# Two more weight blocks in flight at the first hand-over of a weight stream, and an output bias added on TensorE

## What is computed

```
x = x + gat2(elu(gat1(layernorm(x))))          # gat1: 8 heads of 768, W1 (768, 6144); gat2: W2 (6144, 768)
t = layernorm(x)
probs = softmax(t @ Wg + bg)                   # 8 experts, the best one is used
comb = one_hot(argmax(probs)) * max(probs)
h = gelu(t @ W1[e] + b1[e])                    # W1 (8, 768, 3072)
y = h @ W2[e] + b2[e]                          # W2 (8, 3072, 768)
ffn = sum over e of y * comb[e]
v = clip(ffn @ Wv + bv, -3, 3)                 # one number for each node
scores = sigmoid(t @ Wm + bm); mask = scores >= k-th largest
gr, gi = diagonal of (T(v) - i I)^-1           # tridiagonal, by continued fractions
feats = clip(stack(gr, gi) * mask, -10, 10)
out = x + ffn + bk_scale * (feats @ Wo + bo)
```

## Time and profile before

| | |
|---|---|
| median of 3 runs | 510.85 us (510.09 to 513.81) |
| the profiled execution | 510.67 us |
| its span, from first to last instruction | 508.9 us |
| mean granted clock of TensorE | 0.991 |
| TensorE busy with matmuls | 466.9 us (92%) |
| HBM read | 189.62 MB, 373 GB/s over the span |

### The profile page before, as it was taken

How to read it: one execution, slowest core, us unless ns; L and a number is a source line. 1 busy time by engine, 2 the same in 40 slices (tenths; PEclk the granted TensorE clock), 3 DMA queues, 4 the chain that set the end, 5 groups by cost and what they waited for, 6 DMA issues and landing times.

```text
span 508.9 us, 6128 instructions
## 1 busy us (share of the span) xinstructions
PE 466.9 (92%) x2322; PEld 232.5 (46%) x2322; DVE 136.3 (27%) x362; ACT 62.2 (12%) x115; POOL 34.6 (7%) x53
## 2 busy tenths in 40 slices
PE   7999999999999999999999999897898789789881
PEld 6666665666567344354353443252243225224361
DVE  6664696437117110010020110020010002001165
ACT  1110211012003022020020110120020011002000
POOL 3342240000000211000000000000000000000000
PEclk9999999999999999999999999999999999999996
DMA  8889998876999899999999999999999999999800
GB/s 309 299 305 403 401 400 297 289 257 253 429 426 420 316 405 422 426 424 422 424 427 425 423 424 427 424 422 428 426 421 425 427 423 424 426 427 422 373 1 31
DMA packets 32571, 190.22 MB, mean 374 GB/s; under 512 B 5454, under 2 KB 5662, under 8 KB 18220
## 3 DMA queue, kind: packets, MB, share of 16 engines
q1 hardware_dynamic: 31692, 189.94, 92.1%
q0 software_dynamic: 576, 0.06, 0.1%
q10 hardware_dynamic: 288, 0.03, 0.0%
HBM read 189.62 MB, written 0.39 MB: 373 GB/s over the span
## 4 chain that ended last, share of the span: by engine, by line
PE 59%; DMA 19%; SPq 13%; DVE 6%; issue 2%; ACT 1%; POOL 0%; DVEq 0%; POOLq 0%
PE ps L1227 14%; PE ps L1254 13%; DMA chunk<-in_L_ffn_W 13%; PE ps L1017 11%; PE ps L1057 11%; SPq L353 10%; DMA lower<-in_L_ffn_W 6%; SPq L348 3%; PE ps L1240 2%; PE ps L1045 2%; PE ps L1072 2%; PE ps L1197 1%; PE ps L987 1%; PE ps L1302 0%; DVE elu_y L659 0%
## 5 line engine op out<-in xcount | busy, mean ns | idle before, releaser
L1227 PE MATMUL ps<-chunk,gathered 128*64 128x512 f32 x576 | 131.6, 598 | 17.8 <-DMA chunk<-in_L_ffn_W 17.6
L1254 PE MATMUL ps<-lower,hidden 128*64 128x384 f32 x768 | 131.8, 491 | 7.1 <-DMA lower<-in_L_ffn_W 7.1
L1254 PEld LDWEIGHTS ps<-lower,hidden 128*64 128x64 f32 x768 | 52.5, 136 | 72.7 <-issue 57.7
L1227 PEld LDWEIGHTS ps<-chunk,gathered 128*64 128x64 f32 x576 | 38.4, 136 | 99.2 <-issue 64.8
L1017 PE MATMUL ps<-slot,xT 128*128 128x384 f32 x192 | 64.0, 487 | 0.0
L1057 PE MATMUL ps<-slot,eluT 128*128 128x384 f32 x168 | 55.3, 486 | 0.0
L844 DVE TENSOR_TENSOR biased<-ps,b_T 128x384 f32<-128x384 f32 x32 | 17.1, 555 | 136.4 <-PE ps L1240 136.4
L1017 PEld LDWEIGHTS ps<-slot,xT 128*128 128x128 f32 x192 | 35.6, 190 | 22.6
L1057 PEld LDWEIGHTS ps<-slot,eluT 128*128 128x128 f32 x168 | 31.5, 190 | 20.7
L852 DVE TENSOR_SCALAR place_top<-slot_no,rank,small 128x128 f32<-128x128 f32 x8 | 2.8, 346 | 138.8 <-PE ps L1277 138.8
L505 ACT ACTIVATE hidden<-biased 128x384 f32<-128x384 f32 x32 | 16.3, 523 | 79.8 <-DVE biased L844 79.8
(11 more groups left out here) (285 smaller groups left out, 245.6 us busy)
## 6 DMA issues: line engine op xcount, KB each, us to landing
chunk<-in_L_ffn_W SPq DMA_DIRECT2D x48, 1536.0 KB, 28.8
lower<-in_L_ffn_W SPq DMA_DIRECT2D x64, 1152.0 KB, 30.3
slot<-in_L_gnn_W SPq DMA_DIRECT2D x31, 1152.0 KB, 12.0
slot<-in_L_gnn_W SPq DMA_DIRECT2D x3, 384.0 KB, 5.4
x_sb<-in_x SPq DMA_DIRECT2D x1, 384.0 KB, 3.2
out<-xc SPq DMA_DIRECT2D x1, 384.0 KB, 2.4
wv_half<-in_L_ffn_Wv SPq DMA_DIRECT2D x2, 96.0 KB
b_rows<-in_L_ffn_b SPq DMA_DIRECT2D x1, 96.0 KB
```

Of the source, the lines that this page charges most:

```text
L1227: last = T.matmul(ps[b * CAP:(b + 1) * CAP, s, 0:BANK], gathered[:, k, :], chunks[k][:, at:at + BANK], start=(k == 0), stop=(k == KT - 1))
L1254: last = T.matmul(ps[c * CAP:(c + 1) * CAP, 4, 0:HB], hidden[:, q, k, b, :], lowers[i][:, k, c * HB:(c + 1) * HB], start=(i == 0 and k == ...
```

## The change

1. Places. Two more places for chunks are laid over vectors of the graph network that are dead by then: `extra0` over `att2_rows` and `gb2_rows`, `extra1` over `rows`, `gb1_rows`, `b1_rows`, `counts`, `mask_bias`, `free_i` and the edge lists. Round 0 uses the places of before. All later rounds use `chunks_on` (extra0, extra1, chunks 0 to 3) and `lowers_on` (the old places of chunks 4 and 5, lowers 0 to 5). The old places of lowers 6 and 7 are free after round 0.
2. Waits. The loads of round 1 are written out ahead of the loop. Loads 0 and 1 wait for the vectors that lie in their place, and load i from 2 on for block i - 2 of round 0. From round 2 on the rule is that of before. Round 0 has semaphores of its own (`lead_in`).
3. Wo and Wv. Their rows are fetched and spread by GpSimd after round 0, into the place of lower 6, and the tiles of the chunk chain go to the place of lower 7. ScalarE scales the Wo rows after the last round instead of after round 0.
4. bo. It is loaded by one more small DMA into row 32 of `b2_sb`, and two matmuls of one row, with bk_scale as the weight, add it to banks 6 and 7 right behind L1326. The scaling of its row and GpSimd's addition to `x1` go, and with them TensorE's wait for it. `WARM[11]` falls from 20 to 12.
5. The last two operations of VectorE wait for the scaled rows and for the bias as well.

```diff
+        lowers_on = [nc.alloc_sbuf_tensor_at(f"lower_on{i}", [P, 3, D], f32, offset=first_slot + chunk_at[4 + i])
+                     for i in range(2)] + lowers[0:6]
...
+        chunks_on = [extra0, extra1] + chunks[0:4]
...
-                        (b2_sb[:, :], b2),
+                        (b2_sb[0:EXPERTS, :], b2),
+                    (b2_sb[BO_ROW:BO_ROW + 1, :], bo),
...
-            def load_round(r, e, first=False):
+            def second_room(i):
+
+                if i == 0:
+                    sp.wait_ge(x_based, 1)
+                    sp.wait_ge(dots2_done, 2)
+                elif i == 1:
+                    sp.wait_ge(att_prob, 3)
+                    sp.wait_ge(spread, HEADS + 2)
+                else:
+                    sp.wait_ge(used, used_after(0) + i - 1)
...
             load_round(0, 0, first=True)
-            with sp.Fori(1, ROUNDS) as r:
+            load_round(1, 1, second=True)
+            with sp.Fori(2, ROUNDS) as r:
                 load_round(r, r)
...
-            spread_pair(HEADS + 2)
-            spread_pair(HEADS + 3)
...
+            pool.wait_ge(used, used_after(0) + LOADS)
+            for j in range(2):
+                pool.dma_start(wo_rows[0:1, j, :], wo[j:j + 1, :]).then_inc(end_rows_in, 16)
+            pool.dma_start(wv_row[0:1, :], wv).then_inc(end_rows_in, 16)
...
-            pool.wait_ge(rows_scaled, 1)
-            G.tensor_tensor(x1[:, :], x1[:, :], wv_rows[:, 1, :], ALU.add).then_inc(x1_done, 1)
+            pool.wait_ge(end_rows_in, 48)
+            G.partition_broadcast(wo_rows[:, :, :].rearrange("p a c -> p (a c)"),
+                                  wo_rows[0:1, :, :].rearrange("p a c -> p (a c)")).then_inc(end_spread, 1)
+            G.partition_broadcast(wv_row[:, :], wv_row[0:1, :]).then_inc(end_spread, 1)
...
+            act.wait_ge(end_spread, 1)
+            act.wait_ge(minus_ready, 1)
+            S.activation(wo_rows[:, 0, :], wo_rows[:, 0, :], ACT.Identity, scale=bk_c[:, :])
+            S.activation(wo_rows[:, 1, :], wo_rows[:, 1, :], ACT.Identity, scale=minus_bk[:, :]).then_inc(rows_scaled, 1)
             act.wait_ge(last_dot, 1)
             take_y(rounds)
...
+            dve.wait_ge(rows_scaled, 1)
             dve.wait_ge(scattered, rounds)
+            dve.wait_ge(bias_added, 1)
...
             pe.wait_ge(first_dot, 1)
-            pe.wait_ge(x1_done, 1)
...
+            for b in range(2):
+                last = T.matmul(ps[:, 6 + b, 0:HB], bk_c[BO_ROW:BO_ROW + 1, 0:1].to_broadcast([1, P]),
+                                b2_sb[BO_ROW:BO_ROW + 1, b * HB:(b + 1) * HB], start=False, stop=True,
+                                skip_group_check=True)
+            last.then_inc(bias_added, 1)
             stay_warm(WARM[11], 0)
```

More of the change, by code:

```diff
@@ L47 @@
 GROUP = 4
-SMALL = 11
+SMALL = 12
+BO_ROW = 32
 GNN_HALVES = 2 * 2 * HEADS
@@ L118, in gnn_moe_kernel @@
         assert top[0] == first_slot + MOE_BYTES
[L120 to L123, removed]
+        after_moe = top[0]
+        lowers_on = [nc.alloc_sbuf_tensor_at(f"lower_on{i}", [P, 3, D], f32, offset=first_slot + chunk_at[4 + i])
+                     for i in range(2)] + lowers[0:6]
+        top[0] = first_slot + lower_at[6]
+        wo_rows = place("wo_rows", [P, 2, D])
+        wv_row = place("wv_row", [P, D])
+        top[0] = first_slot + lower_at[7]
+        tail_tiles = [("cf_w", [CP, CL + 2, 4 * (CL + 2)]), ("cf_v", [CP, CL]), ("cf_t", [CP, 4 * (CL + 2)]),
               ("cf_m", [CP, CH, 16]), ("cf_mm", [2, CH, 16]), ("cf_s", [2, CH, 4]), ("cf_x", [2, 4, 4]),
@@ L128, in gnn_moe_kernel @@
               ("cf_f", [P, CL, 2]), ("cf_pre", [2, GC, GC, 4, 4]), ("cf_px", [2, GC, 4, 2, 4]),
-              ("cf_sx", [2, GC, GC - 1, 4, 4])]])
-        att2_rows, gb2_rows, wo_rows, wv_rows = region([
+              ("cf_sx", [2, GC, GC - 1, 4, 4])]
+        (cf_w, cf_v, cf_t, cf_m, cf_mm, cf_s, cf_x, cf_n, cf_p, cf_b, cf_y, cf_th, cf_q, cf_r, cf_a,
+         cf_d, cf_c, cf_g, cf_e, cf_f, cf_pre, cf_px, cf_sx) = [place(*t) for t in tail_tiles]
+        assert top[0] <= first_slot + lower_at[7] + slot
+        top[0] = after_moe
+        (rows, gb1_rows, b1_rows, counts, mask_bias, free_i, edges_i, edges_f, extra1) = region([
+            [("rows", [1, 2, D]), ("gb1_rows", [2 * HEADS, HB]), ("b1_rows", [2 * QU * EXPERTS, HB]),
+             ("counts", [P, P]), ("mask_bias", [P, P]), ("free_i", [P, P], i32),
+             ("edges_i", [P, 2, EDGES // P], i32), ("edges_f", [P, 2, EDGES // P])],
+            [("extra1", [P, HID])]])
+        att2_rows, gb2_rows, extra0 = region([
             [("att2_rows", [P, 2, D]), ("gb2_rows", [P, 2, D])],
-            [("wo_rows", [P, 2, D]), ("wv_rows", [P, 2, D])]])
+            [("extra0", [P, HID])]])
+        chunks_on = [extra0, extra1] + chunks[0:4]
         x1 = place("x1", [P, D])
@@ L159, in gnn_moe_kernel @@
         ones = place("ones", [P, P])
-        edges_i = place("edges_i", [P, 2, EDGES // P], i32)
-        edges_f = place("edges_f", [P, 2, EDGES // P])
-        gb1_rows = place("gb1_rows", [2 * HEADS, HB])
         gb1_T = place("gb1_T", [P, 3, 2 * HEADS])
-        b1_rows = place("b1_rows", [2 * QU * EXPERTS, HB])
         b1_T = place("b1_T", [P, EXPERTS + 1, QU * KT])
         b1_over = place("b1_over", [P, EXPERTS, QU * KT])
-        b2_sb = place("b2_sb", [EXPERTS, D])
+        b2_sb = place("b2_sb", [BO_ROW + 1, D])
         gate_w = place("gate_w", [P, KT, EXPERTS + 1])
@@ L224, in gnn_moe_kernel @@
         moe_in = [sem(f"moe_in{i}") for i in range(LOADS)]
+        lead_in = [sem(f"lead_in{i}") for i in range(LOADS)]
         up_done = sem("up_done")
@@ L339, in room, with load_round @@
                     sp.wait_ge(used, GNN_HALVES)
-            def load_round(r, e, first=False):
+            def second_room(i):
[7 more added lines that the diff above has]
+                    sp.wait_ge(used, used_after(0) + i - 1)
+            def load_round(r, e, first=False, second=False):
+                upper_homes, lower_homes = (chunks, lowers) if first else (chunks_on, lowers_on)
                 for i in range(LOADS):
@@ L344, in load_round @@
                         room(i)
+                    elif second:
+                        second_room(i)
                     else:
                         sp.wait_ge(used, used_after(r - 1) + i + 1)
+                    landed = lead_in[i] if first else moe_in[i]
                     if i < CHUNKS:
-                        sp.dma_start(chunks[i][:, :], w1[e, i * P:(i + 1) * P, :]).then_inc(moe_in[i], 16)
+                        sp.dma_start(upper_homes[i][:, :], w1[e, i * P:(i + 1) * P, :]).then_inc(landed, 16)
                     else:
@@ L352, in load_round @@
                         view = w2[e, at:at + HB, :].rearrange("(p k) c -> p k c", p=P)
-                        sp.dma_start(lowers[i - CHUNKS][:, :, :], view).then_inc(moe_in[i], 16)
+                        sp.dma_start(lower_homes[i - CHUNKS][:, :, :], view).then_inc(landed, 16)
             load_round(0, 0, first=True)
-            with sp.Fori(1, ROUNDS) as r:
+            load_round(1, 1, second=True)
+            with sp.Fori(2, ROUNDS) as r:
                 load_round(r, r)
@@ L868, in _ @@
                 round_(r)
-            dve.wait_ge(spread, HEADS + 4)
-            V.tensor_tensor_reduce(out=blocks(xc[:, :]), in0=ps[:, 6:8, 0:HB], in1=blocks(wv_rows[:, 0, :]),
+            dve.wait_ge(end_spread, 2)
+            V.tensor_tensor_reduce(out=blocks(xc[:, :]), in0=ps[:, 6:8, 0:HB], in1=blocks(wv_row[:, :]),
                                    scale=1.0, scalar=0.0, op0=ALU.mult, op1=ALU.add,
@@ L1215, in first_ffn, with landed @@
                 for b in range(2):
-                    T.matmul(ps[:, 6 + b, 0:HB], hot_T[:, :], b2_sb[:, b * HB:(b + 1) * HB],
+                    T.matmul(ps[:, 6 + b, 0:HB], hot_T[:, :], b2_sb[0:EXPERTS, b * HB:(b + 1) * HB],
                              start=True, stop=True)
             def round_(r, first=False):
+                upper_homes, lower_homes = (chunks, lowers) if first else (chunks_on, lowers_on)
+                def landed(i):
+                    if first:
+                        pe.wait_ge(lead_in[i], 16)
+                    else:
+                        pe.wait_ge(moe_in[i], 16 * r)
                 def up(k):
-                    pe.wait_ge(moe_in[k], 16 * (r + 1))
+                    landed(k)
                     for s in range(3):
@@ L1227, in up @@
                             last = T.matmul(ps[b * CAP:(b + 1) * CAP, s, 0:BANK], gathered[:, k, :],
-                                            chunks[k][:, at:at + BANK], start=(k == 0), stop=(k == KT - 1))
+                                            upper_homes[k][:, at:at + BANK], start=(k == 0), stop=(k == KT - 1))
                         if k == KT - 1 and s < 2:
@@ L1250, in down @@
                         i = 2 * q + b
-                        pe.wait_ge(moe_in[CHUNKS + i], 16 * (r + 1))
```

(1 more changed line is left out.)

20 lines of the change are left out of this document (6 added, 14 removed).

## The result

The changed kernel takes 514.94 us (median of 4 runs, 514.13 to 515.74) against 510.88 us (median of 4 runs, 510.09 to 513.81). The ratio is 1.0068, 95% interval 1.0037 to 1.0099. The profiled execution took 514.13 us with a span of 512.3 us.

A forecast was written before the change was run, and what follows sets the result against it. The prediction took the load stream up to 483.5 us, then the chunk chain, as the bound. From the median of 510.85 us, -3.85 us for the stall and +0.1 us for waits gave 507.1 us, range 505.9 to 509.4 us.

The forecast's parts named there:

- step 3: Wo and Wv rows fetched and spread after round 0, needed only after the last gelu: hidden, price 0.
- step 4: ScalarE's two scalings after the last gelu hidden with 7 us to spare; nothing waits for POOL's deleted addition: price 0.
- step 1: Hand-over from round 0 to round 1: new places and waits remove the load stream's whole stall, -3.85 us.
- The small load of bo: One more small load on SP near the start: 0.5 us of SP, which fits before TensorE's need, price 0.
- The two bias matmuls: End chain on TensorE: 1.55 us, with the shorter filling 0.34 us less than before in sum, price 0.
- The two new waits ahead of the last operations: Two more waits ahead of L968, both semaphores long set: upper end taken, 0.1 us.
- Rival A: The stall only moves to the next hand-over, at round 2, and the 3.85 us come back: 510.9 us; chance 7%.
- Rival B: Only the first dip closes, as SP, POOL or VectorE releases one block late: gain 1.4 us, 509.5 us; chance 6%.
- Rival D: Slower than before: the stream loses rate through other places or fuller queues; 513.4 us at 2% loss; chance 5%.
- Rival C: The clock falls early in the chunk chain, its four moves run at 1.2 GHz: +0.3 us, 507.4 us; chance 12%.

The follow-up runs named there:

- e1: The changed kernel with one more small GpSimd iota at the very end of its program: 507.30 us against 511.42 us for the kernel before, ratio 0.9896.
- e2: The kernel before with one more GpSimd partition_broadcast, which nobody reads, at the very end of its program: 519.18 us against 511.42 us, ratio 1.0130.
- e4: e1 with the old waits for round 1's loads (load i waits for block i of round 0), new places kept: 510.28 us, ratio to before 0.9970.
- f1: e1 with one block of lead in round 1 instead of two, places kept: 507.13 us against 511.39 us for the kernel before, ratio 0.9909.
- e3: The kernel before with round 1's loads written out on SP ahead of the loop, waits unchanged: 510.72 us against 511.42 us, ratio 0.9989.

## Why the prediction was wrong

**The step that failed.** It is step 3 of the parts, "Wo and Wv rows later", which ended in "The cover is over 250 us, the price 0". That is right for the execution in which the rows are spread: they are ready at 222 us. I asked what the moved broadcasts and the deleted addition of step 4 delay within one execution, and not what they leave behind. Both edits together made a partition_broadcast the last operation of GpSimd, and the next execution then begins with a switch of 8.64 us in which TensorE, VectorE and GpSimd have nothing to do. TensorE comes to its first weights at 15.82 us and not at 8.29 us, 7.5 us later, and everything behind follows. (GpSimd's iota and TensorE's first matmul both come 8.4 us later; 0.9 us come back since the matmuls ahead of the first weights were quicker in this profile, 1.28 against 1.93 us for the group of ten.) The sum with this term: 510.85 - 3.75 + 7.5 = 514.6 us, against 514.94 us measured. e1 takes the term away and e2 puts it into the kernel before (+7.8 us).

**What could have been seen beforehand.** The trace of before has four passages between the two kinds. Two show as the idle times of 8.49 and 8.42 us ahead of partition_broadcast that are put down to no releaser; the two back to tensor_tensor lie within longer waits (82.56 and 18.05 us). They cost little there (VectorE waited 2.0 us for the rows of the first), and so I passed them over. The chain of before begins with GpSimd's iota, which says that an operation of GpSimd at the start would be paid in full. What no row of before shows is that the state lives on into the next execution. The Trainium skill comes close in two places. "GPSIMD Engine Reference", section 2.1 on instruction dispatch, says that GpSimd's code can be loaded at run time and that the first call afterwards pays about 6 us; here it was 6.7 to 11.0 us, and it was paid again at each passage. "Runtime: NRT & Kernel Launch", under `nrt_init` cost, says that a kernel on a runtime that stays open starts from what the previous one left. It names memory and event flags there and not code; e1 and e2 show the same of whatever GpSimd holds. That the switch is a load of code is a reading after the first of these pages; the runs show only its times and what brings it on.

**Point by point.**

- The stream was the bound and its stall went (step 1: -3.85 us). From TensorE's first weights to its last block it was 475.2 us before (483.51 - 8.29) and 471.2 us after (487.03 - 15.82): 4.0 us less. In e1 it is 471.6 us, 3.6 us less. The medians give 3.0 us between e4 and e1, which differ in nothing but the waits, and 4.1 us between before and e1. The mechanism was right; 3.85 us was at most a little too much.
- SP issued the two loads right behind the last one of round 0, and there was no new dip at round 2: 414 GB/s in the window of 205 to 215 us, about 0.2 us of stream. Rows of SP's queue, changed kernel:

```profile
139.29 19.73 SPq L378 DMA_DIRECT2D lower<-in_L_ffn_W  x8
159.68 2.14 SPq L373 DMA_DIRECT2D extra<-in_L_ffn_W  x2
174.07 10.56 SPq L373 DMA_DIRECT2D chunk<-in_L_ffn_W  x4
```

- The small load of bo took 0.25 us of SP's queue at 13.19 us, less than my 0.5 us, and delayed nothing. Right. (The neighbour of 5.01 us, which I called one of thousands of short packets, moves 3 KB, that is 768 words. Nothing hung on it.)
- The two bias matmuls took the 1.55 us of the sum, and TensorE stood idle for 1.89 us behind the filling. (I wrote that the trace of before has no matmul of one row. It has two, L1293, but of one column each.)
- ScalarE's scalings are hidden, and so are the bias and the shorter filling. From the start of the last block to the issue of the store it is 22.58 us before (483.51 to 506.09) and 22.53 us after (487.03 to 509.56). The two new waits ahead of the last operations, which I had put at 0.1 us, cost nothing: L993 ends at 507.44 us and L997 starts at 507.47 us. Timeline of the end, changed kernel, to be read with the earlier trace rows:

```profile
496.00 1.55 PE L1365 MATMUL ps<-b_sb,bk_c 1*128 1x384 f32 x4
497.49 2.94 PE L1016 MATMUL ps<-ident 128*128 128x128 f32 x24
502.32 0.31 PE L1371 MATMUL ps<-cf_s,to_chunks 2*48 2x64 f32 x2 [1.89 <-DVE cf_s L958]
504.89 0.21 PE L1374 MATMUL ps<-cf_a,ident 48*16 48x16 f32 x2 [2.26 <-DVE cf_a L977]
504.95 0.20 PE L1376 MATMUL ps<-cf_a,turn_back 48*16 48x16 f32 x2
506.22 0.60 PE L1379 MATMUL ps<-cf_g,to_nodes 16*128 16x16 f32 x2 [1.06 <-DVE cf_g L986]
```

- Rival A: the 424 GB/s over the hand-over and round 2 exclude it. Rival B: f1 excludes its reason, since one block of lead closes all dips. Rival D named the right sign, but its mechanism is absent: the stream has 424 GB/s as before.
- Rival C did not come: the clock was up at L1330's counterpart in all nine profiles, and that takes 0.31 us in each. Its price was read from a row that cannot show it. I took L1338's 0.60 us beside L1330's 0.31 us for the price of the lower clock, but the two have different shapes, and L1338's counterpart ran at the lower clock in all nine profiles (0.60 or 0.61 us), so how much of this is the clock stays open. The pair between them, L1333 and L1335, ran at either level. Here it is in the kernel before, at 0.50; its counterparts in the changed kernel, at 1.00, stand above:

```profile
501.39 0.23 PE L1333 MATMUL ps<-cf_a,ident 48*16 48x16 f32 x2 [2.26 <-DVE cf_a L950]
501.46 0.21 PE L1335 MATMUL ps<-cf_a,turn_back 48*16 48x16 f32 x2
```

From the pair's start to the start of L1338 it is 1.34 or 1.35 us in the three profiles with the lower clock at the pair (before, e1, e3), and 1.32 or 1.33 us in the six others, where the clock was up when the pair began: 0.02 us for the pair. The clock fell about 2 us after the filling's end in the profile of before; in the changed kernel it was still up 4.5 us after (filling over at 500.43 us). Windows of the changed kernel:

```profile
504.00:505.00 1.00, 0.11 (x4) 0.11 (x4) 0.73 (x6) 0.00 (x0) 0.00 (x0) 1.00 0.00 0
506.00:507.00 1.00, 0.60 (x2) 0.49 (x2) 0.31 (x2) 0.00 (x0) 0.00 (x0) 0.50 0.00 0
```

The fall did move, then, and across the pair it was worth 0.02 us.

**What comes of it.** e1_iota_last is the changed kernel with its side effect taken out. It beats the kernel before by 1.0% (ratio 0.9896) and the changed kernel by 1.5%. f1 is as fast with one block of lead. It kept both places; that one of them could go to other use follows from its waits, and was not tried.

## What to carry to other kernels

A program that is run again and again begins in the state in which it ended. Where an operation is moved or deleted at the end of an engine's program, ask what the engine is left with, and what the first operation of the next execution needs; where both need the same, the switch is free, and where not, a tiny operation of the right kind at the end pays for the next start while nobody waits. An idle time of many microseconds without a releaser that comes back whenever an engine changes its kind of operation is a cost with a name still to be found, even where it is hidden today. And when a streamed kernel hands one set of places over to the next, one spare block can be worth the whole stall, as it was here, if the loads behind it are freed as fast as before.

## What the runs showed of the hardware

- GpSimd took 6.65 to 11.04 us to pass between iota or tensor_tensor and partition_broadcast, in either direction (26 passages that show as bare idle time in nine profiles, median 8.7 us), and memsets and DMA issues did not need it. What was there at the end of one execution was there at the start of the next of the same program (e1, e2). What another program in between would leave was not tried.
- TensorE may lose time ahead of a stream that it must free, at no cost, while the lead lasts. In e1 the granted clock was 0.50 (1.2 GHz) in the whole window of 163 to 168 us, and TensorE began round 1 at 205.17 us, 3.4 us later than in the kernel before (201.80 us in its timeline). The stream did not sink, and ended 3.3 us earlier than before:

```profile
163.00:168.00 5.00, 5.00 (x22) 3.22 (x23) 3.50 (x23) 0.47 (x1) 0.00 (x0) 0.50 1.01 425
```

- A matmul of one row (1 x 384, four records) took 1.55 us, as much as one of eight rows.
